# A decoder layer's mixer stage: projections in split reduced precision, another order of work, one inverse root a period, and attention's preparation moved into the mixer's end

## The reference

```python
xn = layernorm(x, ln_gamma, ln_beta)
k, v, r = xn @ Wk, xn @ Wv, xn @ Wr
td, tf = sigmoid(time_decay), sigmoid(time_first)
kv = k * v
csum = cumsum(kv * td ** t_idx, axis=time)
wkv = tf * kv + td * shifted(csum)        # shifted by one token, zero first
mixer = (sigmoid(r) * wkv) @ Wo
# attention: q = x @ Wq, k = context @ Wk, v = context @ Wv, 8 heads of 64
# softmax(q k^T / 8) v, then @ Wout + bout
```

## Time and profile before

| quantity | value |
| --- | --- |
| median of 3 runs | 2158.6 us (2155.66 to 2159.18) |
| the profiled execution's own time | 2157.45 us |
| its span in the trace | 2155.7 us |
| PE busy | 2007.5 us (93%) |
| DVE busy | 1505.7 us (70%) |
| POOL busy | 1487.6 us (69%) |
| ACT busy | 1255.8 us (58%) |
| mixer, first projection to last normalisation | 25.75 to 274.01 us |
| attention's first scores | 305.39 us |

### The profile page before, as it was taken

The page is one execution under the profiler, slowest core; times in us unless marked ns, Lnnn a source line. Parts: engine busy times, 40 slices in busy tenths (PEclk is TensorE's granted clock), DMA queues, the critical chain, the costliest instruction groups (busy, mean ns, idle before and its releaser), DMA issues. The chain is left out here.

```text
span 2155.7 us, 51639 instructions
## 1 busy us (share of the span) xinstructions
PE 2007.5 (93%) x14104; PEld 1747.0 (81%) x14104; DVE 1505.7 (70%) x3607; ACT 1255.8 (58%) x3472; POOL 1487.6 (69%) x1739
## 2 busy tenths in 40 slices
PE   5999859999999999975999999999999999579998
PEld 2555548888888788765999999999999999558886
DVE  3666636877878778764677778888888888335554
ACT  2555446665666666632677777777777777324443
POOL 2666521577776767674577778888888888459764
PEclk9999979999999999997999999999999999789999
DMA  4300013233242242322767777677777777366642
GB/s 130 98 0 0 0 44 128 80 109 128 78 146 89 78 156 78 98 70 65 232 227 241 233 233 229 230 235 236 233 233 234 234 234 234 122 228 234 197 167 98
DMA packets 244902, 329.87 MB, mean 153 GB/s; under 512 B 50074, under 2 KB 167234, under 8 KB 244836
## 3 DMA queue, kind: packets, MB, share of 16 engines
q1 hardware_dynamic: 218788, 279.97, 40.3%
q0 software_dynamic: 26048, 49.10, 6.2%
HBM read 236.17 MB, written 77.18 MB: 145 GB/s over the span
## 5 line engine op out<-in xcount | busy, mean ns | idle before, releaser
L1191 POOL DMA_INDIRECT slot_token<-a_entry,a_slot_i x256 | 263.2, 1028 | 112.1 <-issue 71.6
L1687 POOL DMA_INDIRECT part_rows<-e_out,e_dest x184 | 210.7, 1145 | 74.0 <-issue 66.0
L1820 ACT ACTIVATE e_sg<-e_g 128x256 f32<-128x256 f32 x368 | 141.8, 385 | 197.9 <-PE e_g L1512 197.5
L1679 POOL DMA_INDIRECT e_xg<-x_rows,e_tok x188 | 196.6, 1046 | 85.9 <-issue 56.2
L1869 DVE TENSOR_TENSOR e_h<-e_sg,e_u 128x256 f32<-128x256 f32 x368 | 157.9, 429 | 94.1 <-PE e_u L1512 40.4
L1011 ACT ACTIVATE a_prob<-a_s,a_ntop 128x128 f32<-128x128 f32 x512 | 180.9, 398 | 0.9 <-DVE a_ntop L1382 0.7
L1695 POOL TENSOR_TENSOR e_wd1l<-e_raw_d,e_wd1h 128x256 fp32r<-128x256 f32 x184 | 145.4, 826 | 18.2 <-ACT e_wd1h L1800 17.6
L1695 POOL TENSOR_TENSOR e_wd0l<-e_raw_d,e_wd0h 128x256 fp32r<-128x256 f32 x184 | 146.1, 830 | 14.2 <-ACT e_wd0h L1800 13.5
L1884 DVE TENSOR_SCALAR e_out<-e_d,e_dest 128x256 f32<-128x256 f32 x184 | 80.7, 480 | 95.6 <-PE e_d L1512 95.6
L1512 PE MATMUL e_d<-e_wd1h,e_ht1h 128*128 128x256 f32 x368 | 109.2, 297 | 24.5 <-issue 24.5
L866 PE MATMUL a_o<-a_wo,a_ot 128*128 128x256 f32 x512 | 123.2, 384 | 8.3 <-DVE a_ot L1449 8.3
(11 more groups left out here) (332 smaller groups left out, 7464.6 us busy)
## 6 DMA issues: line engine op xcount, KB each, us to landing
e_raw_g<-in_eg SPq DMA_DIRECT2D x94, 512.0 KB
e_raw_u<-in_eu SPq DMA_DIRECT2D x94, 512.0 KB, 5.5
e_raw_d<-in_ed SPq DMA_DIRECT2D x93, 512.0 KB
part_rows<-a_zero SPq DMA_DIRECT2D x16, 2048.0 KB
f_part<-part_rows SPq DMA_DIRECT2D x16, 2048.0 KB, 9.5
x<-in_x SPq DMA_DIRECT2D x16, 512.0 KB, 3.6
x_rows<-x SPq DMA_DIRECT2D x16, 512.0 KB
out_rows<-f_res SPq DMA_DIRECT2D x16, 512.0 KB, 9.9
```

The costliest lines, as they stand in the source:

```text
L1191: pool.indirect_dma_start(k.slot_tok, bass.IndirectOffsetOnAxis(ap=slot_i[:, j, q:q + 1], axis=0), entry[:, j, q, :], None, bounds_check=S ...
L1679: pool.indirect_dma_start(xg[a][:, n, :], None, k.x2_d, bass.IndirectOffsetOnAxis(ap=tok[a][:, n, 0:1], axis=0))\
L1687: pool.indirect_dma_start(k.part_d, bass.IndirectOffsetOnAxis(ap=dest[a][:, n, 1:2], axis=0), out[a][:, n, :], None).then_inc(put[a], 16)
L1820: act.activation(sg[m % 2][:], bank_g[m % 2][:, 0:SETW], ACT.Silu).then_inc(sg_rdy, 1)
```

## The change

In the mixer the k, v and r weights are multiplied by gamma once and split into high and low float32r parts; beta's contribution becomes a constant offset per output feature, computed by 12 one-column products (`offsets`, on PE, into `m_bk`, `m_bv`, `m_br`), that the keys' copy, the gate's sigmoid and `keyed` add. `turned` now writes only the high part of the transposed rows, and DVE makes the low part (`turned_low`, two instructions a period). `m_xnt` and `m_y` are double, by the group's parity. Both roots of a period (group g+2's input, group g-2's output) are one chain on 8 columns (`root`). `norm_in` runs two groups ahead. PE's order in a period is project half 0, turn, project half 1, both halves of mix. In the last period ACT, DVE and POOL also make attention's splits (`high_ahead`, `low_ahead`, `context_low`), and PE projects attention's keys and values of group 0 before and after the last `mix` (`project_ahead`). Attention starts without them. The other edits (the setup's semaphores joined, `k.ct` kept from the mixer on, attention's buffers of even and odd groups swapped) add no instruction.

```diff
+        parts = {n: [p.sb(f"w{n}{h}", [P, DC, D], F32R) for h in "hl"] for n in "kvr"}
+        offset = {n: p.sb("b" + n, [P, DC]) for n in "kvr"}
...
+        AHEAD_BANKS = [("k", 0, bank_t[0]), ("k", 1, bank_t[1]), ("k", 2, bank_k), ("k", 3, bank_r),
+                       ("v", 0, bank_v[0]), ("v", 1, bank_v[1]), ("v", 2, bank_t[0]), ("v", 3, bank_t[1])]
...
         def periods(eng, period):
-            period(0)
-            period(1)
-            with eng.Fori(2, NG - 1) as g:
-                period(g)
-            period(NG - 1)
+            period(0, 0)
+            period(1, 1)
+            with eng.Fori(1, NG // 2 - 1) as i:
+                period(2 * i, 0)
+                period(2 * i + 1, 1)
+            period(NG - 2, 0)
+            period(NG - 1, 1)
...
+                        high, low = parts[n]
+                        cols = slice(c * P, (c + 1) * P)
+                        split_product(pe, bank[:], [((high[:, q, cols], low[:, q, cols]), (xnt[par][0][:, q, :], xnt[par][1][:, q, :]))
+                                                    for q in range(DC)]).then_inc(kvr_done, 1)
...
+                def period(g, par):
+                    project(g, par, 0)
                     if more(g):
                         turn(g + 1)
+                    project(g, par, 1)
                     if at_least(g, 1):
-                        mix(g - 1, 1)
+                        mix(g - 1, 1 - par, 0)
+                        mix(g - 1, 1 - par, 1)
...
+                offsets()
                 turn(0)
-                pe.wait_ge(w_in, DMA + 64)
+                pe.wait_ge(low_rdy, ONE + LOWS)
                 periods(pe, period)
-                mix(NG - 1, 0)
-                mix(NG - 1, 1)
+                project_ahead(range(2))
+                mix(NG - 1, 1, 0)
+                mix(NG - 1, 1, 1)
+                project_ahead(range(2, 8))
...
-                def period(g):
+                def period(g, par):
                     keys(g, 0)
+                    if not more(g):
+                        high_ahead("k")
+                        high_ahead("c")
                     gate(g, 0)
                     if more(g):
-                        norm_in(g + 1)
+                        turned(g + 1, 1 - par)
+                    else:
+                        high_ahead("q")
+                        high_ahead("v")
                     keys(g, 1)
+                    gate(g, 1)
+                    if more(g, 2):
+                        norm_in(g + 2)
                     if at_least(g, 2):
                         norm_out(g - 2)
-                    gate(g, 1)
-                    if more(g):
-                        turned(g + 1)
...
+                def weights_high():
+                    act.wait_ge(w_in, DMA + 64)
+                    for n in "kvr":
+                        for c in range(DC):
+                            act.activation(parts[n][0][:, c, :], w[n][:, c, :], ACT.Identity, scale=k.gam[:, c:c + 1])\
+                               .then_inc(high_rdy, 1)
                 norm_in(0)
-                turned(0)
+                weights_high()
+                turned(0, 0)
+                norm_in(1)
+                act.wait_ge(low_rdy, ONE + LOWS)
                 periods(act, period)
+                empty_ahead(range(2))
                 norm_out(NG - 2)
+                empty_ahead((2, 3, 6, 7))
                 norm_out(NG - 1)
...
+                def root(n, first, last):
+                    if last > TG:
+                        pool.wait_ge(mv2_rdy, ONE + MOMENTS * (n - OUT + 1))
+                        if at_least(n, OUT + 1):
+                            pool.wait_ge(x1_rdy, ONE + n - OUT)
+                    if first < TG:
+                        pool.wait_ge(mv_rdy, ONE + MOMENTS * (n + 1))
+                        if at_least(n, 1):
+                            pool.wait_ge(xn_rdy, ONE + n)
+                    cols = slice(first, last)
                     apart(pool, k.past_pool)
-                    pool.tensor_scalar(ve_t[:], mv_t[:, :, 1], EPS, None, ALU.add).then_inc(ve_s, 1)
-                    pool.tensor_scalar(nm_t[:], mv_t[:, :, 0], -1.0, None, ALU.mult).then_inc(ve_s, 1)
-                    pool.tensor_tensor(rs_t[:], ve_t[:], k.mhalf[:], ALU.pow).then_inc(rs_s, 1)
-                    pool.tensor_tensor(off_t[:], nm_t[:], rs_t[:], ALU.mult).then_inc(off_s, 1)
-                def rstd_in(g):
-                def rstd_out(g):
+                    pool.tensor_scalar(ve[:, cols], mv[:, cols, 1], EPS, None, ALU.add).then_inc(rs_rdy, 1)
+                    pool.tensor_scalar(nm[:, cols], mv[:, cols, 0], -1.0, None, ALU.mult).then_inc(rs_rdy, 1)
+                    pool.wait_ge(rs_rdy, ONE + 4 * n + 2)
+                    pool.tensor_tensor(rs[:, cols], ve[:, cols], k.mhalf[:, cols], ALU.pow).then_inc(rs_rdy, 1)
+                    pool.wait_ge(rs_rdy, ONE + 4 * n + 3)
+                    pool.tensor_tensor(off[:, cols], nm[:, cols], rs[:, cols], ALU.mult).then_inc(rs_rdy, 1)
...
+                def gated(g, par, c):
                     pool.wait_ge(wkv_rdy, ONE + DC * g + c + 1)
                     pool.wait_ge(sr_rdy, ONE + DC * g + c + 1)
-                    pool.wait_ge(o_done, ONE + 2 * g)
-                    pool.tensor_tensor(y[:, c, :], run[:, c, :], sr[:, c, :], ALU.mult).then_inc(y_rdy, 1)
-                def period(g):
-                    if more(g):
-                        rstd_in(g + 1)
+                    if at_least(g, 2):
+                        pool.wait_ge(o_done, ONE + 2 * (g - 1))
+                    pool.tensor_tensor(y[par][:, c, :], run[:, c, :], sr[:, c, :], ALU.mult).then_inc(y_rdy, 1)
+                def period(g, par):
                     decayed(g, 0)
-                    if at_least(g, 2):
-                        rstd_out(g - 2)
+                    root(g + 2, 0 if more(g, 2) else TG, 2 * TG if at_least(g, 2) else TG)
+                    if not more(g):
+                        context_low()
                     decayed(g, 1)
-                    gated(g, 0)
-                    gated(g, 1)
-                rstd_in(0)
+                    gated(g, par, 0)
+                    gated(g, par, 1)
+                root(0, 0, TG)
+                root(1, 0, TG)
                 periods(pool, period)
-                rstd_out(NG - 2)
-                rstd_out(NG - 1)
+                root(NG - 2 + OUT, TG, 2 * TG)
+                root(NG - 1 + OUT, TG, 2 * TG)
...
-                    dve.tensor_tensor(kv[:, c, :], kc[:, c, :], bank_v[c][:], ALU.mult).then_inc(kv_rdy, 1)
+                    dve.scalar_tensor_tensor(kv[:, c, :], bank_v[c][:], offset["v"][:, c:c + 1], kc[:, c, :],
+                                             ALU.add, ALU.mult).then_inc(kv_rdy, 1)
...
+                def turned_low(g, par):
+                    for c in range(DC):
+                        dve.wait_ge(xnt_rdy, ONE + DC * g + c + 1)
+                        dve.tensor_tensor(xnt[par][1][:, c, :], bank_t[c][:], xnt[par][0][:, c, :].bitcast(F32),
+                                          ALU.subtract).then_inc(xl_rdy, 1)
...
-                def period(g):
+                def period(g, par):
                     if at_least(g, 2):
+                        residual(g - 2, 0)
                         residual(g - 2, 1)
+                        moments_out(g - 2)
+                    keyed(g, 0)
+                    if more(g, 2):
+                        moments_in(g + 2)
+                    if not more(g):
+                        low_ahead("k")
+                        low_ahead("c")
+                    summed(g, 0)
+                    keyed(g, 1)
                     if more(g):
-                        moments_in(g + 1)
-                    keyed(g, 0)
-                    if at_least(g, 2):
-                        moments_out(g - 2)
-                    summed(g, 0)
-                    if at_least(g, 1):
-                        residual(g - 1, 0)
-                    keyed(g, 1)
+                        turned_low(g + 1, 1 - par)
+                    else:
+                        low_ahead("q")
                     summed(g, 1)
                 moments_in(0)
+                moments_in(1)
+                weights_low()
+                turned_low(0, 0)
+                dve.wait_ge(low_rdy, ONE + LOWS)
                 periods(dve, period)
+                residual(NG - 2, 0)
                 residual(NG - 2, 1)
+                low_ahead("v")
                 moments_out(NG - 2)
                 residual(NG - 1, 0)
                 residual(NG - 1, 1)
                 moments_out(NG - 1)
+                empty_ahead((4, 5))
...
-                act.wait_ge(k.wp_in, 8 * 16)
-                weights_high("q")
-                context_high(0)
-                weights_high("k")
-                weights_high("v")
                 for b in range(TG):
                     for f in range(3):
```

(6 more changed lines are left out.)

253 lines of the change are left out of this document (154 added, 99 removed).

## The result

| | before | after |
| --- | --- | --- |
| median of 4 runs each, beside one another | 2157.73 us (2155.66 to 2159.18) | 2135.31 us (2134.28 to 2136.5) |
| ratio, 95% interval | | 0.9892 [0.9878, 0.9907] |
| span of the profiled execution | 2155.7 us | 2132.7 us |
| DVE's first `m_kv` of group 2 (K) | 58.70 | 57.02 |
| the same of group 15 | 248.67 | 239.96 |

What follows compares the result with a forecast made beforehand. PE bounded the mixer before; after the change the loop of DVE with POOL would, at 13.85 us a period. From 2157.45 us, -10.9 - 2.9 - 14.4 = -28.2 gave 2129 us, range 2111 to 2138.

Steps and rivals of the forecast that it cites:

- term 1: Mixer's steady period on PE: with split products PE's bound is 12.5 us, 2.1 us below the period before.
- term 2: Mixer's loop on DVE and POOL: period 13.85 instead of 14.61 us, with a stalled second scan; -10.9 us together.
- term 3: Mixer's start, up to K of group 2: 55.8 instead of 58.70, -2.9 us.
- term 4: Mixer's end, from K of group 15 to attention's first scores: 42.3 instead of 56.7 us, -14.4 us.
- rival 1: Mixer's loop is looser and PE is the bound: period 12.5 to 13.2 us, time 2111 to 2120; chance 0.20.
- rival 2: Mixer's period stays at 14.6: power doubles, one more DVE stall of 0.4; 2138 or 2141 us; chance 0.13 with Rival 4.
- rival 3: Mixer: PE's waits drop its granted clock, period 16.6 us, time 2166, slower than before; chance 0.04.
- Rival 4: Mixer's end grows by what attention's start loses: term 4 near -4, time 2139; chance 0.13 together with rival 2.

Runs made afterwards that it cites:

- e8: Changed kernel with POOL's gate product waiting for both decay products, moments one step from their residual, and banks' emptying shared between ACT and DVE: 2117.12 us, ratio 0.9804.
- the first experiment: Changed kernel with POOL's gate product of half 0 held until both decay products are done: 2120.96 us, ratio 0.9819.
- e5: Changed kernel with two of each mixer projection's six products (low weight by high input) left out: 2138.68 us in one execution.
- e10: e8 with the same two of six products left out of each mixer projection as in e5: 2110.8 us, ratio 0.9776.

## Why the prediction was right, and where it was off

**PE's period (term 1), 0.2 short.** I wrote 12.5 as PE's bound; where PE waits for nothing it is 12.73 (the first periods of after, and all but the first two of e8). Starts of float32r records are 0.2335 apart instead of 0.228 (36 of them, 8.40), the first record behind the transposes takes 0.1 longer to the next start and the one behind mix 0.2, and mix (3.26 from 114.43 to the next start in e8) and transposes (0.79) are a little shorter than written. In after it did no harm, as the loop closes later there; in e8 it is the period.

**The loop (term 2), right in mechanism, 0.3 us short a period.** This is the mis-sized term that makes most of the miss (3.9 of 5.3 us). Against K = 113.88 the first scan starts at 2.31 (2.44 written), the power at 4.51 (4.62) with 1.67 (1.69), the second decay product at 6.42 (6.6), the second scan at 7.74 (7.9), its second line at 10.08 (10.2). Up to there I was 0.12 too slow. Then the step that failed: "two residuals 0.60 each, the output's moments 1.77". The residuals take 1.20, but the moments wait for the semaphore of the second one and start 1.66 behind the first in place of 1.20. That is +0.46, and 14.16 instead of 13.85. Over 12 periods 0.31 makes 3.7 of the 3.9 that the term missed (-7.0 instead of -10.9); moving the moments gave 0.39 a period back. In the kernel before, other work stood between a residual and its moments in every period, so none of its steady rows shows the wait.

**Which part brings the stall.** The prediction said "Now the doubled `m_y` bites". The size was right (2.30 written, 2.30 measured, in every second scan), the reason only for three early periods: with a single `m_y` they lose the stall, and it is back from 104.75 on. The rows put it down to a mix that is over early because PE draws ahead; this is argued and not shown by a run. That the two instructions meet there, and what it costs, is settled by the first experiment. The Trainium skill (SBUF — State Buffer, "Who interferes with whom") calls this an exclusive lock of a shared port pair, taken by who comes first; 2.30 for 1.225 fits it, and `m_ve` at 0.96 beside the first scan, against 0.23 alone (on 4 columns, at 257.17), is the other direction. The runs show that the overlap costs this; that ports are the reason, no run here can show.

**The start (term 3), 1.2 short.** K of group 0 came at 32.97 instead of 32.4. Among the experiments with six products, whose edits lie behind it, it moved between 32.5 and 34.6. Period 0 was 10.18 (10.2 written). Period 1 was 13.87 instead of 13.2: its first decay product stands behind the last gate product of group 0 on POOL, `m_ve` is stalled there to 1.20, PE's values come 0.29 late, and the wait at the moments is 0.26.

**The end (term 4), right:** -14.2 for -14.4. On DVE two errors offset each other in part: up to the scan of half 0 it took 3.78 where the terms make 4.22, and from the query split to the second scan 3.23 where they make 2.50. That is luck. The larger parts came as written: mix ends at K + 19.2 (19.0 written), the ahead jobs at 26.1 (25.9), the last normalisation at 28.65 (28.8), the scores at 42.5 (42.3). The clock after PE's wait of 4.07 us, windows, is to be held against the earlier trace rows:

```profile
254.00:258.00 4.00, 3.98 (x12) 3.31 (x13) 3.41 (x11) 0.00 (x0) 0.67 (x3) 0.63 0.01 2
...
270.00:274.00 4.00, 2.50 (x11) 1.93 (x12) 1.38 (x2) 1.19 (x2) 3.92 (x11) 0.58 0.39 130
```

One part was mis-sized without harm to the sum: I wrote that "about 4.7 stick out" of the key and value jobs. Their removal lets the mixer end 2.46 earlier.

**The rivals.** The looser loop (rival 1) isn't there in after, but 1.08 and 0.39 of waiting are all that parts after from it (12.69 is left, in the rival's 12.5 to 13.2). A period that stays (rival 2) needed 0.4 on another stall beside a doubled power; the stall came, 0.46, at another place, while the power stayed at 1.67. The clock (rival 3) was 1.00 through the periods in spite of PE's waits of 1.05; with more idle time on PE it did fall, to 0.93 between 150 and 250 us in e5. Rival 4 fell with the end's parts.

## What to carry to other kernels

When a change takes an engine off the path, lay out the next loop instruction by instruction, and look at which two engines' instructions will then meet: here one wait more on GpSimd, which costs something only in the last group, was worth 14 us of 2135. In a hand-written order put a step between an instruction and the next one of its own engine that waits for its result. And before cutting an engine's work because it sets the period, look for the limit behind it: here TensorE was full and set the period, and with 2.8 us of its work taken out of each period the period fell by only 0.04 us, to the loop behind it.

## What the hardware showed that I had not expected

- BATCH_NORM_STATS2 directly behind the TENSOR_TENSOR whose semaphore it waits for, on the same engine, stands idle 0.26 to 0.38 us in the periods of after, with a start 0.34 to 0.46 later than the issue distance; one step away the wait is gone.
- A power on GpSimd costs 1.04 us on 4 columns and 1.67 on 8, after 0.557 on one. Two of 4 columns, one behind the other, take 2.10 with the step to the next, one of 8 takes 1.74.
- A GpSimd product of 1.30 us that starts 0.07 us ahead of the scan (121.55 and 121.62) lengthens the scan by 1.08 us.
- TensorE's own period (12.73) and that of the loop of VectorE and GpSimd (12.69) can lie so close that cutting the one leaves the period where it was.
- With a third of the projections' records left out (e5) TensorE's granted clock was 0.93 between 150 and 250 us, against 1.00 with all of them; with the same records left out of the faster order (e10) it was 1.00 in every stretch from 32 to 216 us.
